# Statistics and normalisation of the next batch element's x moved behind the statistics of the first FFN output tile, in a fused attention and FFN kernel

## The chip, the cores and the metric

The kernel runs on one core of one Trainium2 chip. The metric is device time in microseconds (us); lower is better. Before the change three runs gave a median of 2429.0 us (2428.91 to 2429.45).

## What is computed

Sixteen batch elements of 512 x 512 float32 go through an attention layer and a quantised FFN, each with a normalisation before and after it and a residual:

```python
x = x + layernorm(attention(layernorm(x)))   # 16 heads of 32, ALiBi, causal, low-rank q and kv
x = x + layernorm(ffn(layernorm(x)))         # fp4 weights, 512 -> 2*1408 -> 512

def ffn(x):
    gate, up = split(x @ w_gate_up.T)
    y = (silu(gate) * up) @ w_down.T
    return y / sqrt(mean(y * y) + 1e-6)
```

## The kernel before

Every engine runs its own instruction stream, written out by hand, and semaphores join the streams. `step(t, att, ffn, nxt)` stands once per engine; it does the attention of batch element t (if `att`) and, woven into it, the FFN of element t-1 (if `ffn`). `nxt` says that element t+1 is prepared too. There are seventeen steps: t = 0 has attention and the preparation of the weights, t = 1 to 15 have both, t = 16 the FFN alone; `nxt` holds for t = 0 to 14.

The middle of a step is a loop over 64 slots (`SLOTS`), which all engines go through in the same order. In a slot TensorE makes score products (L550, L567) and a few of the FFN's products into `dense` banks (L379); the other engines handle what came out of slots a little earlier. From slot 41 on, two transposed score tiles e are made in a slot. What matters there:

- **TensorE**: after every fourth tile e, `values(s)` (L583) multiplies the probabilities of group s (four heads, one tile of 128 keys) by V. It waits for the semaphore `keep`, count s + 1. `values(6)` is issued in slot 47, `values(7)` in slot 49.
- **ScalarE**: exponentials of the tiles (L770); copy of a finished FFN output tile i from PSUM into `stage` (`y_copy`, L708). The first two are done in slots 43 and 48.
- **GpSimd**: `keep_causal(s)` (L1323) zeroes the probabilities above the diagonal and releases `values(s)`. `keep_causal(6)` stands in slot 46, `keep_causal(7)` in slot 48. The helper `power` (L1190) raises variances to the power -0.5; it waits for the semaphore `ve`, and GpSimd works in program order, so whatever follows waits as well. `y_add(i)` (L1266) adds the residual to an output tile. In step 0 GpSimd also scales blocks of weights (`unit`, L1203).
- **VectorE**: `y_moments(i)` (L828, L835, L1021 to L1026) takes the statistics of output tile i, `y_norm(i)` (L1032, L1035) normalises it after its `power`. The statistics of the next x (`moments`, the same L828 and L835, and `ask_rstd`, L937) read `xin`, as does its normalisation (`normalise`, L839, four tiles). `o_split` (L972, L974) splits an attention output. In step 0 `unit` (L906, L909) rounds and splits weights.
- **SyncE**: issues the DMAs: the statistics rows `mrow` that the later score tiles need, x of the next element, the finished output tiles.

The tables that set the places of the moved work are `LN1_SLOT, LN1_POWER, LN1_NORM = 43, 45, 46`: statistics of x in slot 43, its power in slot 45, one tile normalised in each of slots 46 to 49. Work on output tile 0 stands in slots 44 (`y_moments`), 45 (`power`), 46 (`y_norm`) and 47 (`y_add`); for tile 1 in slots 49, 50, 51 and 52. In a slot of the GpSimd stream the order is `keep_causal`, power of x, `unit`, `y_add`, power of the output tile.

The order in which VectorE increments `ve` and GpSimd `rs` is a count over both kinds of work, so the waits name the place in that count.

Of the kernel before, what the change touches and what calls it, by code (L numbers as in the profile page):

```python
# [62 lines left out]
NS = len(SLOTS)  # L63
LN_SUMS, LN_SPLIT, LN_ROWS, LN_COPY = (16, 41), (16, 42), (19, 43), (20, 44)
LN2 = 0.6931471805599453
LN1_SLOT, LN1_POWER, LN1_NORM = 43, 45, 46

# [36 lines left out]
def units_of(slot):  # L106

    return [u for u in range(UNITS) if UNIT_SLOT[u] == slot]
# [12 lines left out]
def up_done(m, up):  # L121

    return done(GU_PRODUCTS * (2 * m + up + 1))
# [7 lines left out]
def layer_program(nc, x, wq_down, wq_up_t, wkv_down_t, k_up_t, v_up_t, wo_t, gu_packed, gu_scales,  # L131
# [6 lines left out]
    with ctx:  # L138
        def sb(name, shape, dt):
            return ctx.enter_context(nc.sbuf_tensor(name, shape, dt))  # L140
# [75 lines left out]
        rs = {n: sb("rs_" + n, [P, NT], f32) for n in ("ln1", "ln2", "ln3", "lo")}  # L216
# [20 lines left out]
        def mx_bank(k):  # L237

            return spare[k % 4] if k < AHEAD else low_bank[k % 2]

        sem = {n: ctx.enter_context(nc.semaphore("s_" + n)) for n in COUNTS}
# [27 lines left out]
        def val(name, t, k):  # L269

            pre, n0, nb, n_last = COUNTS[name]
            if isinstance(t, int) and t == 0:
                return pre + k
            if isinstance(t, int) and t == B:
                return pre + n0 + nb * (B - 2) + n_last + k
            return nb * t + (pre + n0 - nb + k)
# [531 lines left out]
        def _(dve):  # L808
            chain = [0]

            def link(t, ins):

                chain[0] += 1
                ins.then_inc(sem["chain"], 1)

            def apart():


                dve.sem_inc(s_passed_v, 1)

            def linked(t):
                dve.wait_ge(sem["chain"], chain[0] if t is None else val("chain", t, chain[0]))
# [76 lines left out]
            def unit(u):  # L899

                bank_ = dense[u % RING][:, :].rearrange("p (a b) -> p a b", a=4)
                if u in ACT_UNITS:
                    dve.wait_ge(s_prep_hi, KC + act_units(u))
                else:
                    dve.wait_ge(s_prep_mm, KC + u + 1)
                    nc.vector.tensor_scalar(unit_dst(u, 0), bank_, 1.0, None, ALU.mult).then_inc(s_own_hi, 1)  # L906
                    dve.wait_ge(s_own_hi, u + 1 - act_units(u))
                groups = KC - 1 if u < 2 * MI else 4
                nc.vector.scalar_tensor_tensor(unit_dst(u, 1), bank_[:, 0:groups, :], 1.0, unit_dst(u, 0)[:, 0:groups, :],  # L909
                                               ALU.mult, ALU.subtract).then_inc(s_prep_lo, 1)  # L910

            def step(t, att, ffn, nxt):
                j = jobs(t)
                chain[0] = 0
                n_ve = [0]
# [111 lines left out]

                def y_norm(i):

                    dve.wait_ge(sem["rs"], val("rs", t, n_y[0] + i + 1))  # L1030
                    q, rstd = ve["lo"][:, i:i + 1], rs["lo"][:, i:i + 1]
                    link(t, nc.vector.scalar_tensor_tensor(q, mv["lo"][:, i, 0:1], rstd, ve["ln2"][:, i:i + 1],  # L1032
                                                           ALU.mult, ALU.add))
                    linked(t)
                    nc.vector.tensor_scalar(stage[:, i % 2, :], stage[:, i % 2, :], rstd, q,  # L1035
                                            ALU.mult, ALU.subtract).then_inc(sem["yn"], 1)
# [72 lines left out]
                    for c in range(KC):  # L1109
                        low("X2", c, x2t[:, 1, c, :], S_X, x2t[:, 0, c, :])  # L1110

                n_y = [3 if nxt else 2]
                if not att:
                    for m in range(MI):
                        gate(m)
# [12 lines left out]
                for slot, (low_tiles, exp_tiles) in enumerate(SLOTS):  # L1128
                    for k in low_tiles:
                        wide = P * (k % NT + 1)  # L1130
                        dve.wait_ge(sem["mx"], val("mx", t, k + 1))
                        apart()
                        nc.vector.tensor_tensor_reduce(out=mx_bank(k)[:, 0:wide], in0=mx_bank(k)[:, 0:wide],  # L1133
                                                       in1=mmax[:, L - wide:L], scale=-1.0 / S_SCORE, scalar=3e38,
                                                       op0=ALU.add, op1=ALU.min,
                                                       accum_out=ncol[:, k:k + 1]).then_inc(sem["low"], 1)
                    if isinstance(t, int) and t == 0 and slot:
                        for u in units_of(slot - 1):
                            unit(u)
                    if slot == LN_SUMS[1]:  # L1140
                        guess_logs(1)
                    if slot == LN_SPLIT[1]:
                        finish_logs(1)
                    for e in exp_tiles:
                        if e % (HG * NT) == HG + 1 and e > HG * NT:
                            o_split(e // (HG * NT) - 1)
                    if ffn:
                        for m in range(MI):
                            if m and slot == up_done(m, 0) + 2:
                                gate(m)  # L1150
                            if slot == up_done(m, 1) + 2:
                                if m:
                                    up(m)
                                h_high(m)
                        for i in range(NT):
                            if slot == down_done(i) + 4:
                                y_norm(i)
                            if slot == down_done(i) + 2:
                                y_moments(i)
                    if nxt and slot == LN1_SLOT:  # L1160

                        dve.wait_ge(sem["xin"], val("xin", t, 16))
                        moments(t, "ln1", lambda i: xin[:, i, :], range(NT))
                        ask_rstd("ln1")
                        n_ln1 = n_ve[0]
                    if nxt and LN1_NORM <= slot < LN1_NORM + NT:
                        i = slot - LN1_NORM
                        dve.wait_ge(sem["rs"], val("rs", t, n_ln1))
                        normalise("ln1", xin[:, i, :], xin[:, i, :], i).then_inc(sem["ln1"], 1)
                o_split(NG - 1)  # L1170
                if ffn:
# [8 lines left out]
            for t in range(1, B):  # L1180
                step(t, True, True, t < B - 1)
# [4 lines left out]
        def _(pool):  # L1186
            def power(t, name, k, i0=0, i1=NT):

                pool.wait_ge(sem["ve"], k if t is None else val("ve", t, k))
                nc.gpsimd.tensor_tensor(rs[name][:, i0:i1], ve[name][:, i0:i1], half[:, 0:i1 - i0],  # L1190
                                        ALU.pow).then_inc(sem["rs"], 1)
# [53 lines left out]
            def step(t, att, ffn, nxt):  # L1245
                k = 0
                if ffn:
                    power(t, "ln2", 1)
                    power(t, "ln3", 2)
                    k = 2  # L1250
                n_y = (2 if ffn else 0) + (1 if nxt else 0)

                def h_low(m):

# [71 lines left out]
                if not att:  # L1326
                    for m in range(MI):
                        h_low(m)
                    for i in range(NT):
                        power(t, "lo", n_y + i + 1, i, i + 1)  # L1330
                        y_add(i)
                    return
                if isinstance(t, int) and t == 0:
# [3 lines left out]
                for slot, (low_tiles, exp_tiles) in enumerate(SLOTS):  # L1337
                    if slot == LN_SUMS[0]:
                        guess_logs(0)
                        finish_logs(0)  # L1340
                    for e in exp_tiles:
                        if e % HG == 1 and e > 1:
                            keep_causal(e // HG - 1)
                    if nxt and slot == LN1_POWER:
                        power(t, "ln1", n_y)
                    if isinstance(t, int) and t == 0:
                        for u in range(RING, UNITS):
                            if UNIT_SLOT[u - RING] == slot:
                                unit(u)
                    if ffn:  # L1350
                        for m in range(MI):
                            if slot == up_done(m, 1) + 2:
                                h_low(m)
                        for i in range(NT):
                            if slot == down_done(i) + 5:
                                y_add(i)
                            if slot == down_done(i) + 3:
                                power(t, "lo", n_y + i + 1, i, i + 1)
                keep_causal(NG * NT - 1)
                if ffn:  # L1360
                    for i in range(NT):
                        if down_done(i) + 3 >= NS:
                            power(t, "lo", n_y + i + 1, i, i + 1)
                        if down_done(i) + 5 >= NS:
                            y_add(i)

# [141 lines left out]
```

## Time and profile before

| | before |
|---|---|
| median of 3 runs | 2429.0 us |
| the profiled execution | 2428.72 us |
| its span, first to last instruction | 2427.0 us |
| TensorE matmul busy | 2349.2 us, 97% |
| VectorE busy | 1555.9 us, 64% |
| ScalarE busy | 1400.2 us, 58% |
| GpSimd busy | 669.0 us, 28% |
| mean granted TensorE clock | 0.987 of full speed |
| chain that ended last | TensorE 90%, VectorE 5%, ScalarE 2%, issue 1%, GpSimd 1% |

The span is the time between the first and the last instruction of the program; the execution's own time is 1.7 us longer. "Busy" is the time in which an engine works on at least one instruction. The chain that ended last is followed back from the last instruction, at each step to what released it. A step of the kernel takes 144.8 us, so the same place is found again at that distance in the trace.

### The profile page before, as it was taken

To read this page: it belongs to the slowest core of one execution; us is meant where nothing else is said; L and a number is where in the kernel's file an instruction comes from. 1 tells how busy PE (TensorE), PEld (TensorE's weight loads), DVE (VectorE), ACT (ScalarE), POOL (GpSimd) and SP (SyncE) were. 2 spreads that over 40 slices of the span, in tenths; PEclk is the share of its full clock that TensorE was granted. 3 is DMA by queue.
4 is the path that set the end of the run, shared out by engine and by line. 5 is a ranking of instruction groups with operands and counts; after the bars stand their busy time and mean duration, and the time that the engine had idled before them with its cause. 6 is when DMAs were issued, how large, how long until landed. Compare 5 with 4: busy or idle time off the path is not lost.

```text
span 2427.0 us, 38384 instructions
## 1 busy us (share of the span) xinstructions
PE 2349.2 (97%) x13020; PEld 1081.5 (45%) x13020; DVE 1555.9 (64%) x4344; ACT 1400.2 (58%) x3866; POOL 669.0 (28%) x923
## 2 busy tenths in 40 slices
PE   7699999999999999999999999999999999999988
PEld 3344444444444444444444444444444444444433
DVE  7867575665757666575765757566675765757542
ACT  4757466474656647466564755647475564756610
POOL 5522223132231312223132232312323132232312
PEclk8799999999999999999999999999999999999999
DMA  5020121202112120121202012120121202012000
GB/s 151 19 65 24 36 53 36 70 19 59 30 53 53 36 70 19 38 51 45 61 20 72 17 53 53 37 70 19 45 45 45 61 28 70 18 45 53 19 18 18
DMA packets 99523, 108.89 MB, mean 45 GB/s; under 512 B 22895, under 2 KB 73199, under 8 KB 99311
## 3 DMA queue, kind: packets, MB, share of 16 engines
q1 hardware_dynamic: 98462, 105.65, 16.5%
q8 instruction: 103, 1.69, 0.3%
q10 hardware_dynamic: 864, 0.79, 0.1%
q14 instruction: 94, 0.77, 0.1%
HBM read 38.49 MB, written 16.78 MB: 23 GB/s over the span
## 4 chain that ended last, share of the span: by engine, by line
PE 90%; DVE 5%; ACT 2%; issue 1%; POOL 1%; DMA 0%; SPq 0%; POOLq 0%; DVEq 0%; ACTq 0%
PE dense L379 65%; PE psO L583 6%; PE psO L379 4%; PE score L567 4%; PE low L550 3%; PE score L550 3%; DVE st_ln L828 1%; PE low L567 1%; ACT arena L770 1%; PE low L385 1%; PE low L474 1%; PE score L474 1%; PE score L385 1%; POOL arena L1323 0%; ACT score L687 0%
## 5 line engine op out<-in xcount | busy, mean ns | idle before, releaser
L379 PE MATMUL dense<-arena,wgu 128*128 128x512 f16 x3872 | 920.2, 379 | 1.5 <-DVE arena L931 1.2
L379 PEld LDWEIGHTS dense<-arena,wgu 128*128 128x128 f16 x3872 | 369.7, 97 | 394.0 <-issue 7.7
L379 PE MATMUL dense<-wdn,arena 128*128 128x512 f16 x2112 | 533.7, 379 | 2.6 <-POOL arena L1260 2.6
L1260 POOL TENSOR_TENSOR arena<-late,arena 128x512 f16<-128x512 f32 x176 | 203.4, 1155 | 821.6 <-DVE arena L967 611.9
L1133 DVE CUSTOM_DVE_ANT_0 low<-low,mmax 128x128 f32<-128x128 f32 (+3 forms) x672 | 278.9, 436 | 226.5 <-PE low L550 223.1
L770 ACT ACTIVATE arena<-score 128x512 f32<-128x512 f32 (+3 forms) x720 | 300.4, 437 | 173.6 <-PE score L567 131.2
L687 ACT ACTIVATE low<-low,ncol 128x128 f32<-128x128 f32 (+3 forms) x672 | 299.8, 446 | 121.9 <-DVE ncol L1133 114.7
L687 ACT ACTIVATE score<-score,ncol 128x384 f32<-128x384 f32 x352 | 214.3, 609 | 141.6 <-DVE ncol L1133 141.3
L379 PEld LDWEIGHTS dense<-wdn,arena 128*128 128x128 f16 x2112 | 198.7, 98 | 183.8 <-issue 9.3
L1133 DVE CUSTOM_DVE_ANT_0 score<-score,mmax 128x384 f32<-128x384 f32 x352 | 214.0, 649 | 75.1 <-PE score L550 74.6
L1323 POOL TENSOR_SCALAR_AFFINE_SELECT arena<-arena 128x512 f32<-128x512 f32 x240 | 162.3, 676 | 292.6 <-ACT arena L770 292.6
L567 PE MATMUL score<-qst,kst 128*128 128x512 f16 (+3 forms) x784 | 218.2, 305 | 2.7 <-ACT arena L770 2.5
L583 PE MATMUL psO<-arena 128*32 128x512 f32 (+3 forms) x1920 | 177.9, 443 | 24.1 <-POOL arena L1323 22.4
L972 DVE TENSOR_SCALAR arena<-oc 128x512 f16<-128x512 f32 x64 | 27.6, 431 | 224.6 <-ACT oc L681 222.1
L550 PE MATMUL low<-kst,qst 125*128 125x128 f16 (+3 forms) x672 | 155.5, 278 | 7.7 <-ACT low L687 7.4
L770 ACT ACTIVATE arena<-low 128x384 f32<-128x384 f32 (+3 forms) x240 | 103.5, 431 | 99.1 <-PE low L567 97.1
L672 ACT ACTIVATE late<-dense,gate_scale 128x512 f32<-128x512 f32 x176 | 119.6, 680 | 58.7 <-PE dense L379 38.3
L944 DVE SCALAR_TENSOR_TENSOR late<-late,dense 128x512 f32<-128x512 f32 x176 | 120.5, 685 | 51.4 <-ACT late L672 51.4
L952 DVE SCALAR_TENSOR_TENSOR late<-late,h_scale,dense 128x512 f32<-128x512 f32 x176 | 130.9, 744 | 24.7 <-PE dense L379 24.6
L1133 DVE DVE_READ_ACCUMULATOR2_ANT ncol<- 128x1 f32 x1024 | 145.3, 142 | 0.2
L1190 POOL TENSOR_TENSOR rs_ln<-ve_ln,half 128x4 f32<-128x4 f32 x48 | 49.3, 1026 | 328.2 <-DVE ve_ln L937 323.1
L687 ACT ACTIVATION_READ_ACCUMULATOR low<-low,ncol 128x1 f32 x672 | 132.1, 197 | 0.0
(181 smaller groups left out, 2917.5 us busy)
## 6 DMA issues: line engine op xcount, KB each, us to landing
qst<-arena SPq DMA_DIRECT2D x384, 64.0 KB, 2.0
kst<-arena SPq DMA_DIRECT2D x186, 128.0 KB, 2.6
xin<-x SPq DMA_DIRECT2D x16, 1024.0 KB, 5.1
late<-x SPq DMA_DIRECT2D x64, 256.0 KB, 2.8
out<-late SPq DMA_DIRECT2D x64, 256.0 KB, 2.0
qst<-mrow SPq DMA_DIRECT2D x96, 8.0 KB, 1.9
wgu<-wo_t SPq DMA_DIRECT2D x1, 1024.0 KB, 13.1
wgu<-wq_down SPq DMA_DIRECT2D x1, 768.0 KB, 4.4
```

What stands on the lines that cost most here:

```text
L379: ins = nc.tensor.matmul(dst, w, a, start=first and k == 0, stop=last and k == len(tt) - 1)
L550: nc.tensor.matmul(mx_bank(k)[:, 0:P * (i + 1)], qst[0:P - 3, h, P * i:P * i + P], kst[0:P - 3, h, 0:P * (i + 1)], start=True, stop=True). ...
L567: ins = nc.tensor.matmul(st_bank(e)[:, 0:wide], kst[:, h, P * kt:P * kt + P], qst[:, h, P * kt:L], start=True, stop=h >= STEEP)
L583: ins = nc.tensor.matmul(psO[HD * a:HD * a + HD, P * kt:L], v[:, kt, HD * (HG * g + a):HD * (HG * g + a) + HD], prob_of(s)[:, a, 0:wide], ...
L672: nc.scalar.activation(tb[:, m % 2, :], bank(t, n)[:, :], ACT.Tanh, scale=gate_scale[:, m:m + 1]).then_inc(sem["tanh"], 1)
L687: nc.scalar.activation(mx_bank(k)[:, 0:wide], mx_bank(k)[:, 0:wide], ACT.Exp, scale=-1.0, bias=ncol[:, k:k + 1], accum_out=scol[:, k:k + 1 ...
L770: nc.scalar.activation(prob_of(e // HG)[:, e % HG, 0:wide], st_bank(e)[:, 0:wide], ACT.Exp, scale=1.0 / S_SCORE).then_inc(sem["exp"], 1)
L944: nc.vector.scalar_tensor_tensor(tb[:, m % 2, :], tb[:, m % 2, :], 1.0, bank(t, n)[:, :], ALU.add, ALU.mult).then_inc(sem["freev"], 1)
L952: nc.vector.scalar_tensor_tensor(tb[:, m % 2, :], tb[:, m % 2, :], h_scale[:, m:m + 1], bank(t, n)[:, :], ALU.mult, ALU.mult).then_inc(sem ...
L1133: nc.vector.tensor_tensor_reduce(out=mx_bank(k)[:, 0:wide], in0=mx_bank(k)[:, 0:wide], in1=mmax[:, L - wide:L], scale=-1.0 / S_SCORE, scal ...
L1260: nc.gpsimd.tensor_tensor(ht[:, 1, m, :], tb[:, m % 2, :], ht[:, 0, m, :], ALU.subtract).then_inc(sem["hl"], 1)
L1323: nc.gpsimd.affine_select(out=diagonal, in_=diagonal, compare_op=ALU.is_ge, fill=0.0, base=0, pattern=[[0, HG], [1, P]], channel_multiplie ...
```

## The change

The statistics of the next x move from slot 43 to slot 45, their power from 45 to 47, the four normalisations from slots 46 to 49 to slots 48 to 51. The statistics of output tile 0 (slot 44) now stand ahead of those of x on VectorE, and its power (slot 45) ahead of the power of x on GpSimd. The counts that the waits name follow the new order. No instruction is added or taken away.

```diff
-LN1_SLOT, LN1_POWER, LN1_NORM = 43, 45, 46
+LN1_SLOT, LN1_POWER, LN1_NORM = 45, 47, 48
+
+def norm_of_y(i, nxt):
+    return i + (4 if nxt and i else 3)
+
+def norm_of_x(ffn):
+    return 4 if ffn else 1
...
                 def y_norm(i):
-                    dve.wait_ge(sem["rs"], val("rs", t, n_y[0] + i + 1))
+                    dve.wait_ge(sem["rs"], val("rs", t, norm_of_y(i, nxt)))
...
                     if nxt and LN1_NORM <= slot < LN1_NORM + NT:
                         i = slot - LN1_NORM
-                        dve.wait_ge(sem["rs"], val("rs", t, n_ln1))
+                        dve.wait_ge(sem["rs"], val("rs", t, norm_of_x(ffn)))
...
                     if nxt and slot == LN1_POWER:
-                        power(t, "ln1", n_y)
+                        power(t, "ln1", norm_of_x(ffn))
...
                             if slot == down_done(i) + 3:
-                                power(t, "lo", n_y + i + 1, i, i + 1)
+                                power(t, "lo", norm_of_y(i, nxt), i, i + 1)
```

The lines of the changed kernel stand 8 to 11 lower than those of the kernel before. GpSimd, slots 44 to 50 of a step from 1 to 14, before (L1190 is `power`, L1323 `keep_causal`, L1266 `y_add`):

```order
L1323 AFFINE_SELECT arena<-arena 128x4x128 x4
L1190 TENSOR_TENSOR rs_ln<-ve_ln,half 128x4
L1190 TENSOR_TENSOR rs_lo<-ve_lo,half 128x1
L1323 AFFINE_SELECT arena<-arena 128x4x128
L1266 TENSOR_TENSOR late<-late 128x512
L1323 AFFINE_SELECT arena<-arena 128x4x128 x2
```

The same place after the change:

```order
L1331 AFFINE_SELECT arena<-arena 128x4x128 x4
L1199 TENSOR_TENSOR rs_lo<-ve_lo,half 128x1
L1331 AFFINE_SELECT arena<-arena 128x4x128
L1199 TENSOR_TENSOR rs_ln<-ve_ln,half 128x4
L1274 TENSOR_TENSOR late<-late 128x512
L1331 AFFINE_SELECT arena<-arena 128x4x128 x2
```

The power of x moved from ahead of `keep_causal(6)`, the single AFFINE_SELECT, to behind it; it now stands between that and `y_add(0)`.

VectorE, from slot 42 on of the same step, before (L974 ends `o_split(0)`, `st_ln<-xin` to `ve_ln` are the statistics of x, `st_lo` to `ve_lo` those of output tile 0):

```order
L974 SCALAR_TENSOR_TENSOR arena<-oc,arena 128x512
L828 BN_STATS st_ln<-xin 128x6 x4
L835 BN_AGGR mv_ln<-st_ln 128x2 x4
L937 TENSOR_SCALAR ve_ln<-mv_ln 128x4
L828 BN_STATS st_lo<-late 128x6
L835 BN_AGGR mv_lo<-st_lo 128x2
L1021 TENSOR_TENSOR ve_lo<-mv_lo 128x1
L1023 TENSOR_SCALAR ve_lo<-ve_lo 128x1
L1026 SCALAR_TENSOR_TENSOR ve_lo<-mv_lo,ve_lo 128x1
L1032 SCALAR_TENSOR_TENSOR ve_lo<-mv_lo,rs_lo,ve_ln 128x1
L1035 TENSOR_SCALAR late<-late,rs_lo,ve_lo 128x512
L839 TENSOR_SCALAR xin<-xin,mv_ln,rs_ln 128x512 x3
```

and after the change:

```order
L985 SCALAR_TENSOR_TENSOR arena<-oc,arena 128x512
L839 BN_STATS st_lo<-late 128x6
L846 BN_AGGR mv_lo<-st_lo 128x2
L1032 TENSOR_TENSOR ve_lo<-mv_lo 128x1
L1034 TENSOR_SCALAR ve_lo<-ve_lo 128x1
L1037 SCALAR_TENSOR_TENSOR ve_lo<-mv_lo,ve_lo 128x1
L839 BN_STATS st_ln<-xin 128x6 x4
L846 BN_AGGR mv_ln<-st_ln 128x2 x4
L948 TENSOR_SCALAR ve_ln<-mv_ln 128x4
L1043 SCALAR_TENSOR_TENSOR ve_lo<-mv_lo,rs_lo,ve_ln 128x1
L1046 TENSOR_SCALAR late<-late,rs_lo,ve_lo 128x512
L850 TENSOR_SCALAR xin<-xin,mv_ln,rs_ln 128x512
```

The nine instructions on x's statistics moved behind the five on output tile 0. Of the four normalisations of x, the first now follows `y_norm(0)`, one each follows `y_moments(1)` and `o_split(1)`, and the last follows `y_norm(1)`.

In step 0, GpSimd, slots 44 to 48, before (L1203 is `unit`):

```order
L1203 TENSOR_TENSOR arena<-late 128x2x256
L1190 TENSOR_TENSOR rs_ln<-ve_ln,half 128x4
L1203 TENSOR_TENSOR arena<-late 128x2x256
L1323 AFFINE_SELECT arena<-arena 128x4x128
L1203 TENSOR_TENSOR arena<-late 128x2x256
L1323 AFFINE_SELECT arena<-arena 128x4x128
```

and after the change:

```order
L1212 TENSOR_TENSOR arena<-late 128x2x256 x2
L1331 AFFINE_SELECT arena<-arena 128x4x128
L1199 TENSOR_TENSOR rs_ln<-ve_ln,half 128x4
L1212 TENSOR_TENSOR arena<-late 128x2x256
L1331 AFFINE_SELECT arena<-arena 128x4x128
```

The power of x moved behind `keep_causal(6)` and stands ahead of one `unit` and `keep_causal(7)`.

## Rows read from the trace of the kernel before

**Rows 1.** Waits of TensorE over the whole span: us in total, times, longest us

```profile
PE psO L583 <- POOL arena L1323: 22.4, 16, 5.3
```

**Rows 2.** Timeline of step 7: start us, us, engine, line, operation, count [idle before <-releaser]

```profile
1123.02 0.85 PE L583 MATMUL psO<-arena 128*32 128x384 f32 x8
1123.98 1.04 POOL L1190 TENSOR_TENSOR rs_ln<-ve_ln,half 128x4 f32<-128x4 f32 x1 [2.71 <-DVE ve_ln L937]
1125.48 0.55 POOL L1190 TENSOR_TENSOR rs_lo<-ve_lo,half 128x1 f32<-128x1 f32 x1 [0.45 <-DVE ve_lo L1026]
1125.99 0.63 POOL L1323 TENSOR_SCALAR_AFFINE_SELECT arena<-arena 128x512 f32<-128x512 f32 x1
1126.68 0.64 PE L583 MATMUL psO<-arena 128*32 128x256 f32 x8 [1.18 <-POOL arena L1323]
```

**Rows 3.** Timeline of step 7, GpSimd and TensorE behind that place

```profile
1127.30 1.50 POOL L1266 TENSOR_TENSOR late<-late 128x512 f32<-128x512 f32 x1 [0.68 <-DVE late L1035]
1128.75 0.83 POOL L1323 TENSOR_SCALAR_AFFINE_SELECT arena<-arena 128x512 f32<-128x512 f32 x1
1129.73 0.43 PE L583 MATMUL psO<-arena 128*32 128x128 f32 x8
```

**Rows 4.** Timeline of step 15, where no next x is prepared

```profile
2279.73 0.69 DVE L828 BATCH_NORM_STATS2 st_lo<-late 128x6 f32<-128x512 f32 x1
2281.17 0.16 DVE L1026 SCALAR_TENSOR_TENSOR ve_lo<-mv_lo,ve_lo 128x1 f32<-128x1 f32 x1
2281.86 0.85 PE L583 MATMUL psO<-arena 128*32 128x384 f32 x8
2283.27 1.27 POOL L1266 TENSOR_TENSOR late<-late 128x512 f32<-128x512 f32 x1 [0.68 <-DVE late L1035]
2287.32 0.42 PE L583 MATMUL psO<-arena 128*32 128x128 f32 x8
```

**Rows 5.** Timeline of step 7, VectorE

```profile
1120.70 2.47 DVE L828 BATCH_NORM_STATS2 st_ln<-xin 128x6 f32<-128x512 f32 x4
1123.73 0.17 DVE L937 TENSOR_SCALAR ve_ln<-mv_ln 128x4 f32<-128x4 f32 x1
1126.67 0.55 DVE L1035 TENSOR_SCALAR late<-late,rs_lo,ve_lo 128x512 f32<-128x512 f32 x1
1127.59 1.50 DVE L839 TENSOR_SCALAR xin<-xin,mv_ln,rs_ln 128x512 f32<-128x512 f32 x1
```

**Rows 6.** L1032 over the whole span: ns min/median/max, first and last start us

```profile
L1032 DVE SCALAR_TENSOR_TENSOR ve_lo<-mv_lo,rs_lo,ve_ln x64: 219/569/589, 257.2 to 2422.3; 128x1 f32<-128x1 f32 x64
```

**Rows 7.** Timeline of step 7, VectorE beside a power on GpSimd

```profile
1131.21 0.16 DVE L1026 SCALAR_TENSOR_TENSOR ve_lo<-mv_lo,ve_lo 128x1 f32<-128x1 f32 x1
1131.29 0.54 DVE L839 TENSOR_SCALAR xin<-xin,mv_ln,rs_ln 128x512 f32<-128x512 f32 x1
1131.45 0.86 POOL L1190 TENSOR_TENSOR rs_lo<-ve_lo,half 128x1 f32<-128x1 f32 x1 [0.52 <-DVE ve_lo L1026]
1131.85 0.43 DVE L972 TENSOR_SCALAR arena<-oc 128x512 f16<-128x512 f32 x1
```

**Rows 8.** Timeline of step 0, L972 beside GpSimd's unit

```profile
123.39 2.25 POOL L1203 TENSOR_TENSOR arena<-late 128x512 f32<-128x512 fp8e4 x2 [0.17 <-PE dense L406]
124.05 0.68 DVE L972 TENSOR_SCALAR arena<-oc 128x512 f16<-128x512 f32 x1 [1.33 <-ACT oc L681]
```

**Rows 9.** Timeline of step 0, around the power of x

```profile
114.93 0.68 DVE L906 TENSOR_SCALAR wdn<-dense 128x512 f16<-128x512 f32 x1
115.10 1.04 POOL L1190 TENSOR_TENSOR rs_ln<-ve_ln,half 128x4 f32<-128x4 f32 x1 [4.98 <-DVE ve_ln L937]
116.13 1.05 POOL L1203 TENSOR_TENSOR arena<-late 128x512 f32<-128x512 fp8e4 x1
118.01 0.65 PE L583 MATMUL psO<-arena 128*32 128x256 f32 x4 [5.27 <-POOL arena L1323]
121.69 0.44 PE L583 MATMUL psO<-arena 128*32 128x128 f32 x4
```

More of the change, by code:

```diff
@@ L1110, in step @@
                         low("X2", c, x2t[:, 1, c, :], S_X, x2t[:, 0, c, :])
-                n_y = [3 if nxt else 2]
                 if not att:
@@ L1164, in step @@
                         ask_rstd("ln1")
-                        n_ln1 = n_ve[0]
                     if nxt and LN1_NORM <= slot < LN1_NORM + NT:
                         i = slot - LN1_NORM
-                        dve.wait_ge(sem["rs"], val("rs", t, n_ln1))
+                        dve.wait_ge(sem["rs"], val("rs", t, norm_of_x(ffn)))
                         normalise("ln1", xin[:, i, :], xin[:, i, :], i).then_inc(sem["ln1"], 1)
@@ L1250, in step @@
                     k = 2
-                n_y = (2 if ffn else 0) + (1 if nxt else 0)
                 def h_low(m):
@@ L1357, in step @@
                             if slot == down_done(i) + 3:
-                                power(t, "lo", n_y + i + 1, i, i + 1)
+                                power(t, "lo", norm_of_y(i, nxt), i, i + 1)
                 keep_causal(NG * NT - 1)
@@ L1362, in step @@
                         if down_done(i) + 3 >= NS:
-                            power(t, "lo", n_y + i + 1, i, i + 1)
+                            power(t, "lo", norm_of_y(i, nxt), i, i + 1)
                         if down_done(i) + 5 >= NS:
```

## Prediction

> **What bounds the kernel now.** I first read the waits of TensorE over the span, since only what TensorE waits for can be won by moving work of other engines. One entry is large: L583, the product with V, waits for L1323, the causal select on GpSimd, 16 times and 22.4 us in all [rows 1]. The timeline of step 7 shows one of them. GpSimd raises the variances of x (1123.98, for 1.04 us), then waits and raises those of output tile 0 (1125.48, 0.55 us), and only then runs `keep_causal(6)`, 1125.99 to 1126.62. TensorE starts `values(6)` at 1126.68, after 1.18 us of idleness: it was ready at 1125.50 [rows 2]. The same wait of the same size stands once in each of steps 1 to 14, 144.8 us apart. Step 15, which prepares no x, has the same instructions around this place and no such wait: from its `values(5)` to its `values(7)` it takes 5.46 us, step 7 6.71 us [rows 2 to 4]. So 14 x 1.19 = 16.6 of the 22.4 us are this wait, 5.27 us are one in step 0 [rows 9], and the other 0.5 us are small change.
>
> What the reader is to see: the wait is not for the work of the select but for what stands ahead of it in GpSimd's queue. An order of work costs the time here, not a load.
>
> **The change, step 7 as the pattern of steps 1 to 14.** I rebuild the stretch with the durations of the rows. To bring step 15 onto step 7's clock I subtract 1158.84 us, the distance of the two `values(5)` (2281.86 and 1123.02) [rows 2, 4].
>
> 1. *Output tile 0.* Its statistics start when ScalarE's copy is done, as in step 15: 1120.89, and the last of them ends at 1122.49 [rows 4]. Its power follows 0.08 us later (0.55 us), then `keep_causal(6)` (0.63 us) [rows 2], which ends by 1123.75. TensorE wants it at 1125.50. The wait of 1.18 us goes. Cover: 1.7 us of slack.
> 2. *Statistics of x.* They start where the previous VectorE instruction is about to end, 0.08 us early as L839 behind L1026 does [rows 7]: 1122.41. From their start to L937 it is 3.03 us (1120.70 to 1123.73) [rows 5], so L937 lies at 1125.44 to 1125.61.
> 3. *Power of x.* It starts 0.25 us after L937 starts (1123.73, 1123.98) and takes 1.04 us [rows 2, 5]: 1125.69 to 1126.73. Nothing of TensorE's waits behind it until `y_add(0)` and `keep_causal(7)` are through.
> 4. *Norm of output tile 0.* L1032 starts at 1125.52. Its 0.57 us in the median is a wait for the select beside it; alone it takes 0.22 us [rows 6], so to 1125.74; L1035 to about 1126.33 (0.55 us) [rows 5]. That is ahead of the power's end, so `y_add(0)` starts when the power lets go, 0.04 us before its end, as the select does behind the power: 1126.69. Undisturbed it takes 1.27 us [rows 4]: to 1127.96.
> 5. *First norm of x.* It asks for its SBUF access at about 1126.8, just after `y_add(0)`. In the rows such a pair goes one after the other: an L839 that started beside `y_add(0)` took 1.50 us instead of 0.54, ended 0.28 us after it (1129.09 and 1128.80), and held up `keep_causal(7)`, which ended at 1129.58, 0.78 us behind `y_add(0)` [rows 3, 5, 7]. So here `keep_causal(7)` ends at 1128.73, and `values(7)` starts 0.06 us later (as 1126.68 behind 1126.62): **1128.79**, where it stood at 1129.73 [rows 3].
>
> Each of these steps gives 0.94 us, and the rest of the step moves up with TensorE. It is not the full gain: without any hindrance `values(7)` would start at 1128.48 (2287.32 in step 15) [rows 4]. So some 0.3 us of waiting come back, now at `values(7)` and for `y_add(0)` and `keep_causal(7)`, because the power of x has only moved by one select. 14 x 0.94 = 13.2 us.
>
> *Later in the step.* The two norms of x that now surround `y_norm(1)` push `y_add(1)` by some 0.5 to 0.7 us against TensorE. Behind it stands `keep_causal(10)`, which in the timeline ends well ahead of its product; that slack hides the push, so I cost it at nothing, and without it TensorE would wait again, by what the push exceeds it. The normalised x is needed only by the next step, some 30 us later: nothing. The DMAs of the output tile are issued behind `y_add(0)`, which ends earlier than before: nothing. The statistics rows for the score tiles of slot 48 are issued before any of this: nothing.
>
> *Step 0.* GpSimd waited 4.98 us for the statistics of x and so did everything behind, TensorE for 5.27 us [rows 9]. Now `keep_causal(6)` is free of that, and the wait goes. But VectorE does the two instructions on a weight block first (L906 0.68 us, L909 about the same), so the power of x, before at 115.10 to 116.14, comes 1.4 us later, at 117.5. Behind it stand one `unit` (1.05 us) and `keep_causal(7)` (0.63 us): 119.2. `values(7)` stood at 121.69 [rows 2, 9]; it could not have come before 116.4, and so waits again. Gain 2.5 us, between nothing and 5.27.
>
> **Sum**: 13.2 + 2.5 = 15.7 us off the 2428.72 us of the profiled execution, which lies 0.3 us under the median: 2413.0 + 0.3 = **2413.3 us**.
>
> **The unknown cost.** No row shows the power of x beside a norm of 512 columns on VectorE. One shows the small power (128x1) beside L972: the power got its turn when L839 ended at 1131.83, and L972, which began at 1131.85, took its usual 0.43 us [rows 7]; and L972 is one that GpSimd can hold up, since beside `unit` it took 0.68 us [rows 8]. So a power seems to hold the memory access only briefly, and step 4 is costed without a delay. Bounds: if L1035 holds the power up, the power ends at 1126.33 + 0.98 = 1127.31 (its 1.04 us less 0.06 until it asks) and the gain falls to 0.36 us a step; the other bound is the full 1.25 us of step 15. I take 0.94, as L972 is the nearest row. The Trainium skill, SBUF — State Buffer, section Who interferes with whom, says that of a two-port VectorE operation and a GpSimd operation the one that issues first gets the shared pair for the whole instruction and the other fully blocks. The trace agrees for `y_add` and L839 (1.50 against 0.54 us), but not for the small power and L972. What the rule would give for the large power is the third rival.
>
> **Rivals.**
> - *The norm of x wins the race against `y_add(0)`* (it asks 0.1 us later, which is little). It ends at 1127.31, `y_add(0)` 1.12 us later as in the rows (1127.68 to 1128.80), `keep_causal(7)` undisturbed at 1129.0: gain 0.64 us a step, 9.0 + 2.5, **2417.5 us**. Chance 0.13.
> - *L1035 holds up the power of x*: 0.36 us a step, 5.0 + 2.5, **2421.5 us**. Against it: the power starts first. Chance 0.1.
> - *The power of x holds up L1035 to its end.* L1035 then ends at 1126.73 + 0.28 = 1127.01, the norm of x goes ahead of `y_add(0)` and ends at 1127.47, `y_add(0)` at 1128.6, `keep_causal(7)` at 1129.2: gain 0.47 us, 6.6 + 2.5, **2419.9 us**. For it: the power is already waiting when L1032 ends. Against it: L972. Chance 0.17. It is what the rule of the Trainium skill (SBUF — State Buffer) amounts to here.
> - *Nothing comes back*: two GpSimd operations that now stand ahead of `keep_causal(7)` are short enough, step 0 loses no second wait: 14 x 1.25 + 5.3, **2406 us**. Chance 0.06.
> - *The wait only moves*: `keep_causal(7)` ends about when it did, only step 0 wins: **2426.5 us**. For it: the power of x and `y_add(0)` now stand together ahead of a select that had 0.15 us to spare before (1129.58 to 1129.73) [rows 3]. Chance 0.05.
> - *Slower*: the power of x is held by L1035 (end 1127.31), and `y_add(0)` then by VectorE as long as L839 was by GpSimd (0.96 us): it ends at 1129.5, `keep_causal(7)` at 1130.3, `values(7)` at 1130.33, 0.60 us later than before: 8.4 - 2.5 = 5.9 us lost, **2434.9 us**. It decides from the point where `keep_causal(7)` ends after 1129.67. Against it: it needs both hindrances at their longest. Chance 0.03.
>
> My forecast has 0.46. **The numbers.** The range 2408 to 2422 holds the forecast and the first three rivals, 0.86 in all, less what of them may lie outside. A change of 0.2% (4.9 us) is about what a measurement of this kernel can tell from none. Faster by more than that are the forecast and the first four rivals: 0.92; within it the wait that only moves and part of the last: 0.06; slower 0.02.
>
> **What would show it.** Right: in steps 1 to 14 no wait before `values(6)`, a wait of about 0.3 us before `values(7)`, steps of 143.9 us instead of 144.8, L1035 ending ahead of the power of x, and in step 0 a wait of about 3 us at `values(7)` instead of 5.27 at `values(6)`. Wrong: a wait of 0.7 us or more at `values(7)`; L1035 or the power stretched by half a microsecond; or a new wait of TensorE for a select later in the step, which would mean that the norms of x beside `y_norm(1)` are not covered.

## The result, and the profile after

| | before | changed |
|---|---|---|
| median of 6 runs each | 2428.95 us (2428.42 to 2429.70) | 2416.34 us (2414.68 to 2418.51) |
| the profiled execution | 2428.72 us | 2415.40 us |
| its span | 2427.0 us | 2413.7 us |
| mean granted TensorE clock | 0.987 | 0.987 |

The ratio is 0.9948, with a 95% interval of 0.9936 to 0.9961: 12.6 us faster. The forecast was 2413.3 us, its range 2408 to 2422.

The waits of TensorE over the span of the changed kernel (engine, line waited for: us in total, times, longest us); L594 and L1331 are the product with V and the causal select, L583 and L1323 before:

```profile
PE low L485 <- DVE arena L850: 10.9, 1, 10.9
PE low L561 <- ACT low L698: 8.4, 9, 2.3
PE dense L405 <- DMA wgu<-wq_up_t: 7.7, 1, 7.7
PE score L561 <- ACT score L698: 6.7, 18, 0.5
PE psO L594 <- POOL arena L1331: 5.7, 17, 1.7
```

The entry of [rows 1] fell from 22.4 to 5.7 us. It still has 17 occurrences, one in each step from 1 to 14 among them: the waits shrank and did not vanish. The other four entries stand only in step 0 or, the first of them, in the last step, and none of them is at the place of the moved work.

The timeline of step 7 after the change answers to [rows 2, 3, 5]. Its clock runs 5.63 us behind that of before, by `values(5)` (1117.39 and 1123.02):

```profile
1116.78 2.46 DVE L839 BATCH_NORM_STATS2 st_ln<-xin 128x6 f32<-128x512 f32 x4
1116.95 0.58 POOL L1199 TENSOR_TENSOR rs_lo<-ve_lo,half 128x1 f32<-128x1 f32 x1 [1.29 <-DVE ve_lo L1037]
1117.39 0.85 PE L594 MATMUL psO<-arena 128*32 128x384 f32 x8
1117.49 0.64 POOL L1331 TENSOR_SCALAR_AFFINE_SELECT arena<-arena 128x512 f32<-128x512 f32 x1
...
1119.80 0.64 PE L594 MATMUL psO<-arena 128*32 128x256 f32 x8
...
1120.06 1.02 POOL L1199 TENSOR_TENSOR rs_ln<-ve_ln,half 128x4 f32<-128x4 f32 x1 [1.93 <-DVE ve_ln L948]
1120.13 0.54 DVE L1046 TENSOR_SCALAR late<-late,rs_lo,ve_lo 128x512 f32<-128x512 f32 x1
1121.05 1.27 POOL L1274 TENSOR_TENSOR late<-late 128x512 f32<-128x512 f32 x1
1121.11 1.49 DVE L850 TENSOR_SCALAR xin<-xin,mv_ln,rs_ln 128x512 f32<-128x512 f32 x1 [0.44 <-POOL rs_ln L1199]
1122.27 0.82 POOL L1331 TENSOR_SCALAR_AFFINE_SELECT arena<-arena 128x512 f32<-128x512 f32 x1
...
1123.15 0.43 PE L594 MATMUL psO<-arena 128*32 128x128 f32 x8 [0.23 <-POOL arena L1331]
```

Read it by GpSimd's rows. The power of output tile 0, the select (1117.49 to 1118.13) and only then the power of x: the first product behind the select, `values(6)` at 1119.80, has no wait in brackets any more. The power of x and `y_add(0)` now stand ahead of the next select, and the wait comes back small, 0.23 us at `values(7)`. This row stands at 260.04 in step 1 and at 2130.43 in step 14, so a step takes 1870.39 / 13 = 143.88 us; before it was (2140.72 - 257.84) / 13 = 144.84 by the waits at `values(6)`. The gain is 0.96 us a step.

That makes 13.45 us over the fourteen steps, and the traces differ by 13.3. So step 0, with the start and the end of the program, gave nothing to speak of. Its rows, which answer to [rows 9]:

```profile
109.67 2.06 POOL L1212 TENSOR_TENSOR arena<-late 128x512 f32<-128x512 fp8e4 x2 [0.68 <-PE dense L417]
...
110.79 0.98 DVE L1023 TENSOR_TENSOR mh<-lcol,mh 128x32 f16<-128x32 f32 x1
111.68 0.63 POOL L1331 TENSOR_SCALAR_AFFINE_SELECT arena<-arena 128x512 f32<-128x512 f32 x1
111.70 0.90 DVE L983 TENSOR_SCALAR arena<-oc 128x512 f16<-128x512 f32 x1
...
111.83 0.26 PE L542 MATMUL low<-id,mh 128*96 128x128 f16 x1 [1.68 <-DVE mh L1023]
112.63 0.69 DVE L985 SCALAR_TENSOR_TENSOR arena<-oc,arena 128x512 f16<-128x512 f32 x1
...
113.70 0.68 DVE L917 TENSOR_SCALAR wdn<-dense 128x512 f16<-128x512 f32 x1
...
114.42 0.69 DVE L920 SCALAR_TENSOR_TENSOR wdn<-dense,wdn 128x512 f16<-128x512 f32 x1
...
115.03 2.46 DVE L839 BATCH_NORM_STATS2 st_ln<-xin 128x6 f32<-128x512 f32 x4
...
116.79 0.61 PE L578 MATMUL low<-qst,kst 128*128 128x512 f16 x1 [0.76 <-DMA qst<-mrow]
...
118.30 1.04 POOL L1199 TENSOR_TENSOR rs_ln<-ve_ln,half 128x4 f32<-128x4 f32 x1 [5.99 <-DVE ve_ln L948]
...
119.32 1.05 POOL L1212 TENSOR_TENSOR arena<-late 128x512 f32<-128x512 fp8e4 x1
...
120.33 0.82 POOL L1331 TENSOR_SCALAR_AFFINE_SELECT arena<-arena 128x512 f32<-128x512 f32 x1
...
121.20 0.43 PE L594 MATMUL psO<-arena 128*32 128x128 f32 x8 [1.67 <-POOL arena L1331]
```

and the same places of VectorE and TensorE before the change:

```profile
110.20 0.19 DVE L1012 TENSOR_TENSOR mh<-lcol,mh 128x32 f16<-128x32 f32 x1
110.31 0.42 DVE L972 TENSOR_SCALAR arena<-oc 128x512 f16<-128x512 f32 x1
110.44 0.26 PE L531 MATMUL low<-id,mh 128*96 128x128 f16 x1 [0.89 <-DVE mh L1012]
110.76 0.69 DVE L974 SCALAR_TENSOR_TENSOR arena<-oc,arena 128x512 f16<-128x512 f32 x1
...
111.83 2.46 DVE L828 BATCH_NORM_STATS2 st_ln<-xin 128x6 f32<-128x512 f32 x4
```

Two units of GpSimd (x2, 2.06 us) now follow each other, since the power of x no longer parts them. The second holds up VectorE's last instruction on the statistics rows (L1023: 0.98 us instead of 0.19), and the select behind it holds up L983 (0.90 instead of 0.42). TensorE's wait for those rows grows from 0.89 to 1.68 us. The trace of the changed kernel also runs 0.6 us late at this point, from the first 30 us of the program; that is not the change. The statistics of x start at 115.03 instead of 111.83, 3.2 us later: 0.6 is the late start, 1.3 the hold-up (`o_split(0)` ends 1.9 us later, at 113.32 instead of 111.45), and 1.3 the two instructions on a weight block (L917 and L920) that now stand ahead of them.

The rows also leave later: their three DMAs start at 113.70 instead of 112.31. TensorE, which no longer stands in front of `values(6)`, now waits for them, 0.76 us at 116.79 and 1.66 us in the second trace of the changed kernel (the run `c_change` below); before there was no such wait here. These waits are not what sets `values(7)`, since TensorE waits for the select again before it, 1.67 us in this trace and 2.95 us in the second.

### The profile page after: what moved, and what is told of

Its sections match the earlier page's. It is cut to its first block, busy times and chain, and to the rows that moved or that the text cites. A ratio compares the mean times of both kernels' runs of the same rounds, so it can differ in the third digit from the quotient of the medians.

```text
span 2413.7 us, 38384 instructions
## 1 busy us (share of the span) xinstructions
PE 2349.5 (97%) x13020; PEld 1080.8 (45%) x13020; DVE 1552.6 (64%) x4344; ACT 1399.7 (58%) x3866; POOL 664.5 (28%) x923
## 4 chain that ended last, share of the span: by engine, by line
PE 89%; DVE 4%; ACT 3%; POOL 2%; issue 1%; DMA 0%; SPq 0%; POOLq 0%; DVEq 0%; ACTq 0%
PE dense L390 65%; PE psO L594 6%; PE psO L390 4%; PE score L578 4%; PE low L561 3%; PE score L561 3%; DVE st_ln L839 1%; ACT arena L781 1%; PE low L578 1%; POOL late L1274 1%; POOL rs_ln L1199 1%; PE low L396 1%; PE low L485 1%; PE score L485 1%; PE score L396 1%
## 5 line engine op out<-in xcount | busy, mean ns | idle before, releaser
L1331 POOL TENSOR_SCALAR_AFFINE_SELECT arena<-arena 128x512 f32<-128x512 f32 x240 | 162.3, 676 | 283.6 <-ACT arena L781 283.6
L594 PE MATMUL psO<-arena 128*32 128x512 f32 (+3 forms) x1920 | 177.7, 442 | 7.2 <-POOL arena L1331 5.7
L983 DVE TENSOR_SCALAR arena<-oc 128x512 f16<-128x512 f32 x64 | 28.3, 442 | 216.9 <-ACT oc L692 214.7
## 6 DMA issues: line engine op xcount, KB each, us to landing
wgu<-wo_t SPq DMA_DIRECT2D x1, 1024.0 KB, 13.2
```

Source lines behind the costliest of these rows:

```text
L594: ins = nc.tensor.matmul(psO[HD * a:HD * a + HD, P * kt:L], v[:, kt, HD * (HG * g + a):HD * (HG * g + a) + HD], prob_of(s)[:, a, 0:wide], ...
L1331: nc.gpsimd.affine_select(out=diagonal, in_=diagonal, compare_op=ALU.is_ge, fill=0.0, base=0, pattern=[[0, HG], [1, P]], channel_multiplie ...
```

## The experiments

**The changed kernel again**, on the same chip as the runs of GpSimd's half, of step 0 in the old order and of the power in slot 49.

> The changed kernel again, as the measure for the two runs beside it: 2416 us, the wait of TensorE at values(7) 0.23 us in each of steps 1 to 14.

It took 2416.21 us (2415.06 to 2418.07; before, on the same chip, 2428.88), ratio 0.9948 (0.9936 to 0.9961), with 143.89 us a step and the wait of 0.23 to 0.24 us. Step 0 came out otherwise than in the first trace: the wait at `values(7)` is 2.95 us instead of 1.67, `values(7)` starts at 121.09, and the last products of step 0 start at 138.79, where the kernel before has them at 138.12 and the first trace at 138.23. What differs is the granted TensorE clock (columns: stretch, us, busy us and instructions of PE, PEld, DVE, ACT and POOL, granted clock, DMA share, GB/s). First the first trace, then two rows of the second:

```profile
113.20:120.02 6.82, 5.13 (x21) 2.33 (x21) 6.57 (x16) 3.19 (x10) 1.72 (x2) 0.50 0.02 5
```

```profile
113.20:120.02 6.82, 2.90 (x21) 1.45 (x21) 6.57 (x16) 3.23 (x10) 1.84 (x2) 1.00 0.02 5
121.40:124.80 3.40, 3.40 (x21) 2.39 (x20) 2.30 (x3) 2.36 (x6) 2.49 (x3) 0.50 0.00 0
```

At 0.50, the lower of the clock's two levels (1.2 and 2.4 GHz), the same 21 instructions took 5.13 us instead of 2.90. In the first trace that stretch lies where TensorE would have waited anyway, and its two waits there (0.76 and 1.67 us) are 2.2 us shorter together than those of the second (1.66 and 2.95); in the second trace the stretch at 0.50 lies behind `values(7)`, where TensorE is busy all the time.

**One half each.** Which engine's order makes the gain? First GpSimd's alone:

```diff
-LN1_SLOT, LN1_POWER, LN1_NORM = 45, 47, 48
+LN1_SLOT, LN1_POWER, LN1_NORM = 43, 47, 48
...
-                        power(t, "ln1", norm_of_x(ffn))
+                        power(t, "ln1", 3 if ffn else 1)
...
-                                power(t, "lo", norm_of_y(i, nxt), i, i + 1)
+                                power(t, "lo", i + (4 if nxt else 3), i, i + 1)
```

> Only GpSimd's half of the change: the statistics of x stay in slot 43 ahead of those of output tile 0 on VectorE, but the power of x goes to slot 47, behind keep_causal(6), and the norms to slots 48 to 51. Theory A: the select waited for the power of output tile 0, and that for VectorE, which did x first; so the wait of 1.18 us at values(6) stays in steps 1 to 14 and these steps take 144.8 to 145.1 us (2425 to 2432 us in all, step 0 winning some). Rival: it was the 1.04 us of the power of x on GpSimd that held the select; then the wait shrinks by about 1 us a step, 2414 to 2416 us.

A single run took 2427.90 us. Its timeline of step 7:

```profile
1124.32 0.58 POOL L1199 TENSOR_TENSOR rs_lo<-ve_lo,half 128x1 f32<-128x1 f32 x1 [4.21 <-DVE ve_lo L1037]
1124.87 0.64 POOL L1331 TENSOR_SCALAR_AFFINE_SELECT arena<-arena 128x512 f32<-128x512 f32 x1
...
1125.47 1.02 POOL L1199 TENSOR_TENSOR rs_ln<-ve_ln,half 128x4 f32<-128x4 f32 x1
...
1125.56 0.64 PE L594 MATMUL psO<-arena 128*32 128x256 f32 x8 [1.22 <-POOL arena L1331]
```

GpSimd is idle for 4.21 us ahead of the power of output tile 0, and the wait at `values(6)` is 1.22 us as before. The 1.04 us of the power of x on GpSimd cost nothing: it ran in time in which GpSimd waited for VectorE anyway. A step takes 144.88 us. Theory A holds, the rival falls. In step 0 this run also has a wait of 1.7 us for the statistics rows, as every run with the new order on GpSimd has but the one that moves a unit (1.26 us, last run below), while the runs with the old order there have 0.89 us: the hold-up of L1023 comes from GpSimd's order.

Then VectorE's half alone:

```diff
-LN1_SLOT, LN1_POWER, LN1_NORM = 45, 47, 48
+LN1_SLOT, LN1_POWER, LN1_NORM = 45, 45, 48
...
-                    dve.wait_ge(sem["rs"], val("rs", t, norm_of_y(i, nxt)))
+                    dve.wait_ge(sem["rs"], val("rs", t, i + (4 if nxt else 3)))
...
-                        dve.wait_ge(sem["rs"], val("rs", t, norm_of_x(ffn)))
+                        dve.wait_ge(sem["rs"], val("rs", t, 3 if ffn else 1))
```

> Only VectorE's half of the change: the statistics of x stand behind those of output tile 0, but on GpSimd the power of x stays ahead of the power of output tile 0 and of keep_causal(6) (slot 45). Theory A (a select waits for whatever stands ahead of it): the power of x now waits for statistics that end 1.7 us later (1125.61 instead of 1123.90 on step 7's clock), the power of output tile 0 follows, keep_causal(6) ends at about 1127.9, and the wait at values(6) grows from 1.18 to about 2.4 us in each of steps 1 to 14: 2440 to 2448 us. Rival (VectorE's order alone makes the gain): 2414 to 2418 us.

A single run took 2457.52 us. The mechanism is the one expected, here in step 2, with the waits of 2.41 or 2.42 us in every step from 1 to 14:

```profile
404.98 1.05 POOL L1199 TENSOR_TENSOR rs_ln<-ve_ln,half 128x4 f32<-128x4 f32 x1 [4.41 <-DVE ve_ln L948]
406.00 0.55 POOL L1199 TENSOR_TENSOR rs_lo<-ve_lo,half 128x1 f32<-128x1 f32 x1
406.51 0.63 POOL L1331 TENSOR_SCALAR_AFFINE_SELECT arena<-arena 128x512 f32<-128x512 f32 x1
...
407.20 1.01 PE L594 MATMUL psO<-arena 128*32 128x256 f32 x8 [2.42 <-POOL arena L1331]
```

But the time is 9.5 us above the upper end expected. Fourteen longer waits make 17.2 us and step 0 took 2.1 more; the rest, 9.5 of the 28.8 us between the traces, is the clock: six of the fourteen steps are 1.5 to 1.6 us longer behind that wait than the others. The busy time in stretches of 3.5 us behind that wait, in steps 1, 2 and 3 (columns as above):

```profile
261.10:264.60 3.50, 3.44 (x28) 1.34 (x29) 1.72 (x4) 2.44 (x5) 2.09 (x3) 1.00 0.12 46
407.20:410.70 3.50, 3.50 (x15) 1.06 (x16) 1.30 (x3) 1.57 (x3) 2.08 (x2) 0.52 0.14 52
554.80:558.30 3.50, 3.42 (x28) 1.32 (x28) 1.74 (x4) 2.42 (x5) 2.11 (x3) 1.00 0.11 42
```

In step 2 TensorE got through 15 instructions instead of 28 after the wait, at a granted clock of 0.52. That happened in six of the fourteen steps and in none of those steps of the kernel before or of the changed one. So both halves are needed: VectorE's gives the gain, and without GpSimd's it turns into a loss, since the power of x then waits for statistics that come later and takes the select with it.

**Step 0 alone in the old order.**

```diff
+LN1_OLD = (43, 45, 46)
+def ln1_at(t):
+    return LN1_OLD if isinstance(t, int) and t == 0 else (LN1_SLOT, LN1_POWER, LN1_NORM)
...
-                    if nxt and slot == LN1_SLOT:
+                    if nxt and slot == ln1_at(t)[0]:
```

and so for the other two places.

> The old order in step 0 alone, the new one in steps 1 to 15. Theory A (the traces of the two kernels): in step 0 the gain was given back, because GpSimd's unit now runs straight behind the one before and holds up VectorE's last instruction on the statistics rows, and because TensorE then runs at half clock while it has work. Then the old order in step 0 costs only some 0.5 us: 2416 to 2417.5 us, with the 5.3 us wait at values(6) of step 0 back. Theory B (the prediction's sum): step 0 is worth 2.5 us, so 2418.5 to 2419 us. Steps 1 to 14 as in the changed kernel in both.

It took 2415.26 us (2414.23 to 2416.91), ratio 0.9944 (0.9931 to 0.9956): no slower than the changed kernel at 2416.21, with the wait of 5.27 us back in its trace and 143.89 us a step. Theory B, my 2.5 us, is out: it asked for 2418.5 us at least, and the slowest of the five took 2416.91. The median lies below the range of theory A as well, and 0.95 us below the changed kernel on the same chip, so the runs can't tell a gain of half a microsecond in step 0 from none or from a small loss. The traces scatter as much: from the first `values` with 256 columns to the last products of step 0, the kernel before took 38.2 us, this run with the same order there 38.7, the changed kernel 37.8 and 38.5.

**Power and norms of x behind the next select too.**

```diff
-LN1_SLOT, LN1_POWER, LN1_NORM = 45, 47, 48
+LN1_SLOT, LN1_POWER, LN1_NORM = 45, 49, 50
```

> The power of x two slots later still (49) and the norms of x in slots 50 to 53, statistics in slot 45. Theory A: the wait of 0.23 us left at values(7) comes from the power of x and the norm beside y_add(0), both ahead of keep_causal(7); with them behind it the wait is gone in all 14 steps and the steps are 0.23 us shorter, 3.2 us in all: about 2413 us. Rival: y_add(0) alone sets it, or a later select waits instead: no change within 1 us, with a wait of TensorE for a select at another place.

It took 2409.97 us (2409.64 to 2411.90), ratio 0.9925 (0.9912 to 0.9939). Step 7:

```profile
1117.68 1.27 POOL L1274 TENSOR_TENSOR late<-late 128x512 f32<-128x512 f32 x1 [2.64 <-DVE late L1046]
1118.90 0.63 POOL L1331 TENSOR_SCALAR_AFFINE_SELECT arena<-arena 128x512 f32<-128x512 f32 x1
1119.51 1.03 POOL L1199 TENSOR_TENSOR rs_ln<-ve_ln,half 128x4 f32<-128x4 f32 x1
...
1119.77 0.43 PE L594 MATMUL psO<-arena 128*32 128x128 f32 x8
```

The wait at `values(7)` is gone and the select ends 0.24 us ahead of its product. A step takes 143.58 us, which is all that step 15 had promised (144.84 less 1.25). That is 0.30 us a step under the changed kernel, 4.1 us in fourteen, where I had expected 3.2 us and 2413 us in all. Of the rest of the way from 2416.21, 1.9 us are step 0 with the start of the program (its last products start at 136.93, in the second trace of the changed kernel at 138.79); the granted clock stays at 1.00 there from 90 us on. The same kernel a second time:

> The kernel with the power of x in slot 49 and its norms from slot 50 again, as the measure for the run beside it: 2410 us.

It took 2411.65 us (2410.58 to 2414.56), ratio 0.9930 (0.9917 to 0.9944), again 143.58 us a step. This version is faster than the kernel before by 17 to 19 us and, by the medians on the same chip, than the changed one by 6.2 us (2416.21 and 2409.97).

It also bears on why step 0 is worth so little. Here `values(7)` of step 0 has no wait for a select, at 117.46 instead of 121.69, and yet in both traces of this version the products at the end of step 0 are only 1.05 us ahead of the kernel before (against its place at the start of the stretch). The waits of TensorE over the span show an entry that it did not have before:

```profile
PE dense L417 <- DVE wdn L920: 2.8, 4, 1.6
```

TensorE now waits for VectorE's splits of weight blocks. In this version, with the clock at 1.00, step 0 is bound by the weight work, and what is won at a select is waited for at the next block. In the changed kernel only the first trace has such a wait behind `values(7)`, of 0.63 us.

**Norms of x later, its power not.** What made up the 0.23 us left?

```diff
-LN1_SLOT, LN1_POWER, LN1_NORM = 45, 47, 48
+LN1_SLOT, LN1_POWER, LN1_NORM = 45, 47, 50
```

> The changed kernel with the norms of x two slots later (50 to 53), its power left in slot 47. This splits the 0.23 us left at values(7). If it is the norm of x beside y_add(0), which holds up keep_causal(7) (0.82 us instead of 0.63), the wait shrinks by 0.19 to some 0.04 us a step. If it is the power of x ahead of y_add(0), it stays at 0.23.

```profile
1122.84 0.64 POOL L1331 TENSOR_SCALAR_AFFINE_SELECT arena<-arena 128x512 f32<-128x512 f32 x1
...
1123.53 0.43 PE L594 MATMUL psO<-arena 128*32 128x128 f32 x8
```

The select takes 0.64 us instead of 0.82 and the product starts without a visible wait. A step takes 143.69 us: 0.18 us came from the norm of x beside `y_add(0)` and 0.11 from the power ahead of it. The single time, 2416.81 us, is no lower than the changed kernel's, because step 0 and the last step were longer in this run: the last products of step 0 start at 139.91 instead of 138.23, and in the last step the granted clock was 0.50 for 17.1 us, in the changed kernel's trace for 10.2.

**Step 0: one unit later**, on top of the kernel with the power in slot 49.

```diff
-                            if UNIT_SLOT[u - RING] == slot:
+                            if UNIT_SLOT[u - RING] + (u == 26) == slot:
```

> The same kernel with one edit in step 0: the unit of GpSimd that stood in slot 45 comes behind keep_causal(6), in slot 46. Theory A: it no longer runs beside VectorE's last instruction on the statistics rows, which falls back from 0.98 to 0.19 us, TensorE's wait for it (1.7 us) falls to 0.9, the rows land 0.8 us earlier, and step 0 is up to 0.8 us shorter: 2409 to 2410 us. Rival: step 0 is bound elsewhere by then (weight units on VectorE, TensorE's clock): less than 0.3 us.

It took 2411.44 us (2411.04 to 2413.56), ratio 0.9929 (0.9916 to 0.9941), the same as its measure. The hold-up changed its place:

```profile
110.45 0.63 POOL L1331 TENSOR_SCALAR_AFFINE_SELECT arena<-arena 128x512 f32<-128x512 f32 x1
110.57 0.56 DVE L1023 TENSOR_TENSOR mh<-lcol,mh 128x32 f16<-128x32 f32 x1
...
111.05 1.32 POOL L1212 TENSOR_TENSOR arena<-late 128x512 f32<-128x512 fp8e4 x1
...
111.50 1.42 DVE L985 SCALAR_TENSOR_TENSOR arena<-oc,arena 128x512 f16<-128x512 f32 x1
```

L1023 is now held by the select (0.56 us, not the 0.19 expected) and L985 by the unit (1.42 instead of 0.69). TensorE's wait for the statistics rows fell to 1.26 us only, not to 0.9. Theory A was half right on the cause and wrong on the yield; the rival, that step 0 is bound elsewhere, fits the times.

## Why the prediction was right, and where it was off

- *The cause of the 1.18 us*: right. The select waited for what stood ahead of it, and at the root of that for VectorE's order. The two halves show it: GpSimd's alone left 1.22 us, VectorE's alone made it 2.41.
- *Steps 1 to 14*: 0.94 us a step was forecast, 0.96 measured, 13.45 us against 13.2. The rebuilt timeline held row by row. On the clock of step 7 before, the power of x ran from 1125.69 (forecast 1125.69) and `values(7)` started at 1128.78 (forecast 1128.79); `keep_causal(7)` 0.78 us behind `y_add(0)` was forecast, 0.77 came (1122.32 to 1123.09); a wait of 0.3 us at `values(7)` was forecast, 0.23 came.
- *The unknown cost*: the power of x did not wait and held nobody. It took 1.02 us with L1046 beside it, which took 0.54 us, as alone. So the third rival, and the rule of the Trainium skill as I had applied it (SBUF — State Buffer, Who interferes with whom: the second to issue fully blocks), is not borne out by this trace for the power; it is for `y_add(0)` and L850, 1.49 us instead of 0.54. The race that the first rival turned on went to `y_add(0)`, by 0.06 us (1121.05 and 1121.11).
- *Later in the step*: the norms of x pushed `y_add(1)`, and the slack of `keep_causal(10)` hid it: it ends at 1130.08 and its product starts at 1131.01, 0.9 us later.
- *Step 0*: this is the term that failed. I forecast 2.5 us, "VectorE does the two instructions on a weight block first ... so the power of x ... comes 1.4 us later". It came 3.2 us later (118.30 against 115.10), 0.6 of it the late start of this run. The two instructions cost 1.3 us, as forecast; the other 1.3 us are the hold-up. I had costed the place only by what stands in the queue, not by what the unit that moves up would hold on VectorE. At `values(7)` the gain was 1.1 us: 0.5 as the traces stand (121.69 and 121.20) and 0.6 for the late start. The wait there was 1.67 and 2.95 us, where I had said about 3.
- *The rest of step 0*: I let the whole gain through to its end. There it was 0.5 us in the first trace and a loss of 0.2 in the second (138.79 against 138.12, 0.46 of it a late start). In the first trace two waits behind `values(7)` took it, 0.33 us for a select and 0.63 for a weight block. In the second there is no wait for a weight block, but 3.4 us of work at a granted clock of 0.50, where the kernel before has 0.6 us of it; my estimate is that this costs 1.4 us, half the difference. No run separates the order from the clock here, so why the gain is lost behind `values(7)` stays open.
- *The statistics rows*: I had put them at nothing, "issued before any of this". In steps 1 to 14 that holds. In step 0 they left late and TensorE waited 0.76 and 1.66 us for them; it did no harm only because the select was later still.

The forecast of 2413.3 us was 3.0 us too low. Step 0 with the start and the end of the program makes 2.6 us of that; steps 1 to 14 gave 0.25 us more than forecast; and the profiled execution lies 0.9 us under the median of the changed kernel, where I had added 0.3.

## What to carry to other kernels

When a wait ends at an engine that has little to do, list what stands ahead of the released instruction and ask what each of those waited for. Moving the item with the late input behind the urgent one won most of the wait here, but only when it was moved on both engines: on one alone it won nothing or made the wait longer. A step without the disputed work (here step 15) gives the ceiling, and the distance to it tells whether to move the item one place further. A stretch that other work also binds, as step 0, should be costed by the next wait, not by the one that goes, and by what the work that moves up will stand beside on the other engines.

## What the runs showed that I had not expected

A wait of 2.42 us on an otherwise busy TensorE was followed in six of fourteen cases by about 3.4 us at a granted clock of 0.5, while none of the fourteen waits of 1.2 us in the kernel before was, nor any of the fourteen with GpSimd's half alone. The 1.23 us that each wait had grown by thus cost 26.7 us in steps 1 to 14 instead of 17.2. I can't say from these runs what decides between the six and the eight.
